# Ternary attention: key rows by transposing the key columns, in eight unrolled phases

## What is computed

```python
def bitnet_linear(x, W, b):
    w_scale = jnp.maximum(jnp.mean(jnp.abs(W)), 1e-05)
    qW = jnp.sign(W) * (jnp.abs(W) > 0.5 * w_scale).astype(W.dtype)
    i_scale = jnp.maximum(jnp.max(jnp.abs(x)), 1e-08) / 127.0
    qx = jnp.clip(jnp.round(x / i_scale), -128.0, 127.0)
    out = jnp.einsum('...i,oi->...o', qx, qW) * (w_scale * i_scale)
    return out + b
...
for Wa, ba in ((W_att0, b_att0), (W_att1, b_att1)):
    kv = bitnet_linear(image_embeds, Wa, ba)
    k = jnp.concatenate([kv, kv], axis=-1)
    scores = jnp.einsum('bse,bpe->bsp', fused, k) * inv_sqrt_e
    attn = jax.nn.softmax(scores, axis=-1)
    fused = fused + 0.1 * jnp.einsum('bsp,bpe->bse', attn, k)
```

## Time and profile before

| what | us |
|---|---|
| median of 3 runs (2981.0 to 2986.46) | 2983.72 |
| the profiled execution | 2979.48 |
| its span in the trace | 2977.5 |
| PE busy in the span (88%) | 2610.4 |
| DVE busy (46%) | 1371.2 |
| ACT busy (30%) | 891.1 |

### The profile page before, as it was taken

One profiled execution on the slowest core, in us unless ns is written; L12 is line 12 of the kernel. 1 busy time (PEld: TensorE's weight loads), 2 busy tenths in 40 slices (PEclk: granted clock), 3 DMA queues, 4 the chain that ended last, 5 costly groups with the idle time before them and its releaser, 6 DMA issues. The chain is left out here.

```text
span 2977.5 us, 35940 instructions
## 1 busy us (share of the span) xinstructions
PE 2610.4 (88%) x13417; PEld 1523.8 (51%) x13417; DVE 1371.2 (46%) x1938; ACT 891.1 (30%) x1688; POOL 397.9 (13%) x333
## 2 busy tenths in 40 slices
PE   7899999889999999965798998859976899999993
PEld 4544444334555555433444553537753666676762
DVE  5788888522778877422355222864445100000003
ACT  3645445304533335110121100843331111121210
POOL 0155555300000000012011000000000000000002
PEclk9999999999999999978799999979988899999997
DMA  2022222344544445064400100120000987777752
GB/s 83 29 79 71 87 76 74 103 147 175 178 144 165 155 113 172 16 170 169 169 0 0 39 3 26 61 88 1 0 1 28 372 343 297 296 313 297 305 238 73
DMA packets 83162, 383.92 MB, mean 129 GB/s; under 512 B 14010, under 2 KB 44262, under 8 KB 68314
## 3 DMA queue, kind: packets, MB, share of 16 engines
q1 hardware_dynamic: 66762, 310.78, 28.9%
q0 software_dynamic: 16288, 71.61, 7.1%
HBM read 334.18 MB, written 48.16 MB: 128 GB/s over the span
## 5 line engine op out<-in xcount | busy, mean ns | idle before, releaser
L2600 PE MATMUL psum<-tf_x_T,tf_W 128*128 128x128 f32 x2560 | 291.9, 277 | 7.6 <-DVE tf_x_T L2635 3.8
L2600 PEld LDWEIGHTS psum<-tf_x_T,tf_W 128*128 128x128 f32 x2560 | 288.2, 193 | 18.2 <-issue 18.2
L694 PE MATMUL psum<-ms_context,mb_key_w 128*128 128x361 f32 x768 | 269.3, 487 | 22.6 <-ACT x_rows L604 9.6
L2610 PE MATMUL psum<-tf_W,tt_hidden 128*128 128x512 f32 x640 | 279.9, 596 | 8.0 <-PE psum L2600 8.0
L684 POOL TENSOR_TENSOR x_rows<-ms_state,mb_C_everywhere 128x800 f32<-128x800 f32 x128 | 241.2, 1884 | 312.6 <-DVE ms_state L661 182.4
L2640 DVE TENSOR_TENSOR tf_y<-psum,tf_b 128x512 f32<-128x512 f32 x20 | 13.8, 692 | 572.1 <-PE psum L2610 572.1
L915 PE MATMUL psum<-at_Wv,at_context 128*128 128x512 f32 (+1 forms) x576 | 266.3, 602 | 0.0
L661 DVE TENSOR_TENSOR_SCAN ms_state<-ms_decay,psum 128x800 f32<-128x800 f32 x128 | 232.1, 1814 | 57.4 <-ACT ms_decay L611 41.3
L2624 ACT ACTIVATE tt_hidden<-psum,tf_b 128x128 f32<-128x128 f32 x320 | 91.2, 368 | 486.6 <-PE psum L2600 486.6
L694 PEld LDWEIGHTS psum<-ms_context,mb_key_w 128*128 128x128 f32 x768 | 136.4, 191 | 162.3 <-ACT x_rows L599 64.1
L2610 PEld LDWEIGHTS psum<-tf_W,tt_hidden 128*128 128x128 f32 x640 | 120.2, 190 | 155.0 <-issue 155.0
(11 more groups left out here) (444 smaller groups left out, 3646.9 us busy)
## 6 DMA issues: line engine op xcount, KB each, us to landing
tf_W<-in_L_W SPq DMA_DIRECT2D x40, 4096.0 KB, 13.1
at_piece<-in_L_W_f POOLq DMA_DIRECT2D x24, 1024.0 KB, 6.3
keys_dram<-x_rows SPq DMA_DIRECT2D x128, 180.5 KB, 1.9
at_k_cols<-keys_dram SPq DMA_DIRECT2D x64, 361.0 KB, 3.1
sf_W<-in_L_W SPq DMA_DIRECT2D x16, 1024.0 KB, 7.5
ms_context<-in_ctxT SPq DMA_DIRECT2D x16, 541.5 KB, 4.3
at_context<-in_ctxT SPq DMA_DIRECT2D x8, 1083.0 KB, 5.2
ternary_dram<-at_piece_made POOLq DMA_DIRECT2D x14, 512.0 KB, 4.0
```

The source lines that it names most:

```text
L694: last = nc.tensor.matmul(side[:, 0:SH], lhsT=wk[:, k, e * P:(e + 1) * P], rhs=keys[:, h, k, :], start=(k == 0), stop=(k == KC - 1))
L2600: last = nc.tensor.matmul(up[u][:, m * P:(m + 1) * P], lhsT=w1[j][:, k, (u * GM + m) * P:(u * GM + m + 1) * P], rhs=xT[j][:, k, :], start= ...
L2610: last = nc.tensor.matmul(down[j][:, :], lhsT=hid[j][:, m, :], rhs=w2[j][:, m, :], start=(m == 0), stop=(m == KM - 1))
```

## The change

The row units are no longer computed from `image`. PE transposes them from the finished key columns: 2 transposes of `kT` against the identity per unit in place of 4 matmuls, and DVE's drain becomes a plain copy, since scale and bias are in the columns already. `brow` and its DMA go. A row unit now needs all column units of its phase drained. The loop is gone: all eight phases f are straight-line code, and a is f % 2. Columns of phase f+2 and rows of phase f+1 are made during phase f, so two phases of columns and one of rows are made before the first scores. `average` is split into `turn(f, s)` and `average(f, s)`, with rows between. DVE makes the two queries of a new pair right behind the maxima of the phase before.

The core of the diff (ACT's block follows the same order: `take_cols` of phase f+2, units 0 and 1, behind the exponentials, units 2 to 7 behind the copies of `prob_T`):

```diff
-        brow, kscale = sb("bias_rows", [P, 2, EH]), sb("k_scale", [P, 2])
+        kscale = sb("k_scale", [P, 2])
...
-            sp.dma_start(brow[:, :, :], dram["L1_b_att_rows"].partition_broadcast(P)).then_inc(loaded, 16)
             sp.dma_start(wf[:, :], c.ternary[:, c.ternary.shape[1] - F_ALL:]).then_inc(f_loaded, 16)
...
+            def key_rows(f, units):
+                if f >= PHASES:
+                    return
+                pe.wait_ge(ringT.drained[0], (f + 1) * NT + ringT.n)
                 for u in units:
                     s, t = unitsR[u]
-                    ringR.wait_free(pe, past * NR + u, i, 2 * NR)
-                    for k in range(KD):
-                        last = nc.tensor.matmul(ringR.bank(u)[0:rows_of(t), 0:EH], lhsT=image[:, k, bass.ds(start + (s * S + t * P), rows_of(t))],
-                                                rhs=watt[a][:, k, :], start=(k == 0), stop=(k == KD - 1))
+                    n = rows_of(t)
+                    ringR.wait_free(pe, f * NR + u)
+                    for j in range(2):
+                        last = nc.tensor.transpose(ringR.bank(u)[0:n, j * P:(j + 1) * P], kT[:, s, f % 2, j, t * P:t * P + n], c.ident[:, :])
                     last.then_inc(ringR.filled, 1)
...
+            key_cols(0, range(NT))
+            key_cols(1, range(2))
+            key_rows(0, range(4))
+            key_cols(1, range(2, 5))
+            key_rows(0, range(4, 8))
+            key_cols(1, range(5, NT))
+            key_rows(0, range(8, NR))
+            for f in range(PHASES):
+                scores(f)
+                key_cols(f + 2, range(2))
+                key_rows(f + 1, range(4))
+                turn(f, 0)
+                key_rows(f + 1, range(4, 6))
+                turn(f, 1)
+                key_rows(f + 1, range(6, 9))
+                key_cols(f + 2, range(2, 4))
+                average(f, 0)
+                average(f, 1)
+                key_cols(f + 2, range(4, 6))
+                key_rows(f + 1, range(9, NR))
+                key_cols(f + 2, range(6, NT))
...
-                    nc.vector.scalar_tensor_tensor(kr[0:n, s, a, t, :], ringR.bank(u)[0:n, 0:EH], kscale[0:n, a:a + 1],
-                                                   brow[0:n, a, :], ALU.mult, ALU.add).then_inc(ringR.done(u), 1)
+                    nc.vector.tensor_copy(kr[0:n, s, f % 2, t, :], ringR.bank(u)[0:n, 0:EH]).then_inc(ringR.done(u), 1)
...
-            dve.wait_ge(loaded, 16)
             ringR.grant(dve)
-            take_rows(range(NR), 0, 0)
+            for s in range(2):
+                query(0, s)
+            take_rows(0, range(NR))
+            for f in range(PHASES):
+                for s in range(2):
+                    dve.wait_ge(scored, 2 * f + s + 1)
+                    own(nc.vector.tensor_reduce(neg_max[:, s:s + 1], pair(s), mybir.AxisListType.XY, ALU.max, negate=True))
+                    nc.vector.tensor_scalar(neg_max[:, s:s + 1], neg_max[:, s:s + 1], SC, None, ALU.mult).then_inc(maxed, 1)
+                if f % 2 and f + 1 < PHASES:
+                    for s in range(2):
+                        query(f + 1, s)
+                take_rows(f + 1, range(2))
+                for s in range(2):
+                    dve.wait_ge(exped, 2 * f + s + 1)
+                    own(nc.vector.reciprocal(share[:, s:s + 1], total[:, s:s + 1]))
+                    nc.vector.tensor_scalar(prob[:, s, 0:S], prob[:, s, 0:S], share[:, s:s + 1], 0.1, ALU.mult, ALU.mult).then_inc(shared, 1)
+                    take_rows(f + 1, range(2, 4) if s == 0 else range(4, 9))
+                for s in range(2):
+                    dve.wait_ge(averaged, 2 * f + s + 1)
...
+                take_rows(f + 1, range(9, NR))
```

More of the change, by code:

```diff
@@ L2244, in _, with turn, average @@
-            turn(TURNS - 1, False)
+            def turn(f, s):
+                pe.wait_ge(shared, 2 * f + s + 1)
+                for t in range(ST):
+                    last = nc.tensor.transpose(c.banks[4 + 2 * s + t // 3][:, t % 3 * L:(t % 3 + 1) * L],
+                                               prob[:, s, t * P:(t + 1) * P], c.ident[0:L, 0:L])
+                last.then_inc(turned, 1)
+            def average(f, s):
+                pe.wait_ge(ringR.drained[0], (f + 1) * NR + ringR.n)
+                pe.wait_ge(pT_ready, 2 * f + s + 1)
+                for j in range(2):
+                    for t in range(ST):
+                        last = nc.tensor.matmul(c.banks[4 + 2 * s][:, j * L:(j + 1) * L], lhsT=kr[:, s, f % 2, t, j * P:(j + 1) * P],
+                                                rhs=pT[:, s, t, :], start=(t == 0), stop=(t == ST - 1))
+                last.then_inc(averaged, 1)
@@ L2246, in _, with take_cols @@
         @block.scalar
         def _(act):
-            def take_cols(lo, hi, a, past, i=None):
-                for u in part(NT, lo, hi):
+            def take_cols(f, units):
+                if f >= PHASES:
+                    return
+                for u in units:
                     s, j, z = unitsT[u]
-                    ringT.wait_full(act, past * NT + u, i, 2 * NT)
-                    at = BIAS_AT["att0"] + 2 * a + j
-                    nc.scalar.activation(kT[:, s, a, j, z * SH:(z + 1) * SH], ringT.bank(u)[:, 0:SH], ACT.Identity,
-                                         scale=kscale[:, a:a + 1], bias=bcols[:, at:at + 1]).then_inc(ringT.done(u), 1)
```

154 lines of the change are left out of this document (44 added, 110 removed).

## The result

| | before | after |
|---|---|---|
| median, 5 runs each (before: the three above and two more) | 2983.72 (2981.0 to 2986.86) | 2959.85 (2956.53 to 2967.34) |
| ratio, 95% interval | | 0.9922 (0.9905 to 0.9939) |
| profiled execution | 2979.48 | 2959.85 |
| start of the stage to the first scores | 17.53 | 16.92 |
| first seven phases | 163.08 | 146.27 |

The traces agree with the sign and with most of the steps: the stage lost 16.2 us. The other 7.7 us of the difference of medians are not in the stage: 3.4 us lie in the rest of the span, in lines that the change doesn't touch, and 4.24 us are the distance of the profiled execution before from its median.

A forecast was written before the change was run, and what follows sets the result against it. PE was taken to bound the stage. Terms of -13.2, +0.9 and +0.2 summed to -12.1 us: 2979.48 to 2967.4 on the profiled execution, median 2971.6, range 2965 to 2982.

The forecast's parts named there:

- term 1: First seven phases of the stage: 149.9 us in place of 163.1, so -13.2 us.
- term 2: Start of the stage to the first scores: 18.4 us against 17.53, including 1.6 for one clock fall, so +0.9 us.
- term 3: Scores of the last phase to the last add: 16.7 us against 16.50, so +0.2 us.
- The loop's missing 1.3 us: Old loop turn: laid out at 45.9 us, took 47.19; the difference lies in the loop and straight code loses it.
- Rival 1 and 2: Clock falls once in each of seven phases, 2983, 11%; or stays down over rows, turns and average, 2995, 6%.
- The weighed rule: Transposes alone for 5.4 us per phase: the clock would fall in most phases and nearly all the gain would go.
- Rival 3: Waits dearer than laid out: handovers add 1.6 us, a copy as dear as the old operation 2.5, together 2976; 12%.
- Rival 4: DVE copies cheaper, 0.30 us each: row waits shrink, the stage ends 6 us earlier, 2965.5; 5%.
- Rival 5: The row ring hides wholly: -19.8 us of work with no new wait, 2960; 1%.
- One of the signs: PE waits on DVE of 0.4 to 0.5 us before the third row unit and each turn, 25 to 30 us in all.

The follow-up runs named there:

- the long stretch: Changed kernel with the column units behind the scores and ahead of the average moved behind the average, leaving PE transposes alone from scores to average: 2977.63 us, ratio 0.9987.
- the filling with matmuls: Changed kernel with dummy bf16 matmuls, 12 ahead of the last phase's first turn and 3 ahead of its second: 2958.47 us, ratio 0.9924.
- the new order: Changed kernel with the same work reordered: fewer row units in a burst, rows and columns in turn, no copies before the first scale: 2949.52 us, ratio 0.9895.
- the repeat: The changed kernel measured again without edit, beside the kernel before: 2963.21 us against 2980.26, ratio 0.994.
- The written-out loop: The kernel before with its loop of three turns written out and nothing else changed: 2975.9 us, ratio 0.9986.

## Why the prediction was right in its sign and half its size

The measured gain is 23.9 us, 11.8 more than forecast. **The step that failed** is the one from the stage to the time: "On the profiled execution, 2979.48 becomes 2967.4; the median, 4.24 higher, becomes 2971.6". It put the rest of the span at nothing, and it carried the 4.24 us between one profiled execution and a median of three over to the changed kernel. In its place the runs showed a rest 3.4 us shorter and a profiled execution that lay on its median, together 7.7 of the 11.8 us. The terms of the stage missed by 4.1: 3.6 in term 1, 1.5 in term 2, and 1.0 the other way in term 3. With a stage 16.2 us shorter the same step would have given 2967.5, inside the range.

That rest and offset both fell on the side of the gain was luck of one comparison. The second one gave 17.1 us, with a rest of 2781.3.

**Term 1, the phases: -13.2 forecast, -16.8 measured.** The mechanism was right: two column units, rows in bursts, a wait at each third row unit and before each turn. The sizes were off, each a little:

| from the start of scores, even phase | laid out | measured |
|---|---|---|
| first row unit | 6.12 | 6.09 |
| third row unit | 7.03 | 6.99 |
| first turn | 8.16 | 8.02 |
| second turn | 9.74 | 9.39 |
| columns behind the rows | 11.47 | 11.13 |
| average | 12.69 | 12.36 |
| next scores | 21.7 | 21.31 |

The largest of them is the chain on DVE between the turns. The first turn came 0.14 us earlier than laid out. I put the second 1.58 us behind it, for two copies (0.78), reciprocal (0.18) and scale (0.60); the trace has 1.37. There the reciprocal starts at 2045.40, 0.09 us before the copies' end (2044.73 + 0.76), and the next copies at 2046.10, 0.09 before the scale's end, which lengths added up don't show. With the average (5.34, not 5.41) this is 0.39 us in each of three even phases. In the odd ones the queries cost 0.18 us, not 0.4, which makes 0.61 us in each of three. Phase 6 took 17.9, not 18.5. Together 3.6 us.

**Term 2, the start: +0.9 forecast, -0.6 measured.** PE's rows of the start:

```profile
1978.51 1.40 PE L2181 MATMUL psum<-tn_image_q,tn_w_att 128*128 128x361 bf16 x8 [1.07 <-ACTq L75]
1980.79 6.01 PE L2181 MATMUL psum<-tn_image_q,tn_w_att 128*128 128x361 bf16 x32 [0.87 <-ACT ta_k_cols L2254]
1986.64 0.60 PE L2194 MATMUL psum<-ident,ta_k_cols 128*128 128x128 f32 x4
```

The layout gave 16.8 us, and it took 16.92. PE stood 0.87 us where I expected about 1, and the ten column units and the rest behind it ran at 1.00 (window above). The clock fall for which I added 1.6 us didn't come in this trace, while it did in three other kernels with the same start (the long stretch 18.22, the filling with matmuls 18.24, the new order 18.24) and didn't in five profiles (16.91 or 16.92). It came in three of eight profiles and cost 1.3 us; it belonged in the range and not in the sum.

**Term 3, the end: +0.2 forecast, +1.2 measured.** The chain at full clock was laid out as 14.95 and took 14.86 in the repeat. The half clock cost 2.84 us in the first trace, not 1.75, since it came already under the turns.

**The rest, 7.7 us, is in no term.** It is scatter as far as the runs show it; what makes it vary is open. The same kernel before had medians of 2983.72, 2980.26, 2982.4, 2980.91 and 2981.4 us in its five series, and the span outside the stage varied from 2774 to 2785 us over the profiles. Against a median of about 2981 the gain is 18 to 21 us.

**The loop's missing 1.3 us** was put down to the loop as such. The written-out loop kept all but about 0.2 us of the 1.85 us wait; it was mostly the order.

**The rivals.** Rival 1 and 2, the clock: the stretch with transposes alone (5.04 to 5.16 us in phases 0 to 5, 5.83 in phase 6, busy 3.99) held 1.00 in all seven phases, in both profiles and in three more with the same stretches. The weighed rule, "TensorE: Matmul & The Clock Gate" of the Trainium skill, Part 4, says that transposes don't count as busy work. By it the clock should have fallen in most phases, and it didn't; the row that agreed with it, from 1422.40, showed transposes that failed to raise a low clock, which is another case. But the risk was real and near: with four column units moved, the clock fell in half of the first six phases. Rival 3, dearer waits: not so. A copy as dear as the old operation was priced there at 2.5 us, and 2.2 were measured over six phases. Rival 4, copies of 0.30 us: no, they took 0.42. But they step by 0.34 (two in 0.76), not by 0.39. Rival 5, a ring that hides wholly, was excluded for the bursts, and rightly; with the bursts taken apart it nearly does, and a phase takes the 19.2 us of PE's work alone. That its 2960 is the measured median is chance.

One of the signs was wrong by the prediction's own layout: it asked for 25 to 30 us of waits in all, while its phases hold about 20 (2.5, 2.9 and, in phase 6, 4.2). From start to start they were 17.2.

The range failed because it reached 6.6 us down and 10 up, with the risks of the clock all counted as losses, and with nothing for the scatter of the time before, some 3 us, nor for a layout whose errors all point one way.

## What to carry to other kernels

When a layout is added up from lengths, calibrate it first: take steps from start to start for the same chain on the same engine, since here a sum of lengths was 0.2 us too long in 1.6. When a unit of PE's work gets cheaper than its drain, the gain goes into the ring unless the cheap units are spread one by one between dear ones; spreading them, with fewer copies in front of the scale, took 12.0 us off the seven phases here, where making them cheap had taken 9.3. Judge a wait by starts, since a view that counts gaps behind modelled ends can show none where PE loses 0.3 us each time. Don't carry the distance of one profiled execution from its median over to another kernel; put the scatter of the time into the range. And a wait whose clock fall comes in one execution and not in the next belongs in the range, with its price, not in the sum.

## What the runs showed of the hardware

- f32 transposes of 128x128 start every 0.11 us (four in 0.44 us, 2026.60 to 2027.04 in the new order). Over stretches of 5.04 to 5.16 us with transposes alone, PE busy 3.99, the granted clock stayed at 1.00 in all 30 phases of five profiles. Over 5.83 us with the same busy time it stayed in 14 of 16 and fell in 2, and with 0.55 us more idle time it fell in 3 of 3.
- The same wait with the same instructions around it can cost nothing or 1.3 to 2.8 us by the clock: the 1.89 us in the last phase (14.86 or 17.70 us to the end), the start (16.92 or 18.24), the 1.85 us at a loop turn (0 or 1.7).
- On DVE a `scalar_tensor_tensor` over 128x256 f32 from PSUM took 418 ns with a constant as scalar, exactly as a plain copy, and 478 with the scalar read from a tile. So here the second tensor cost nothing, and the scalar from the tile did.
